# Layer 0's node stage of a four-layer graph network: rows normalized in x's order, and turned in four sets of 64 columns

## What is computed

```
h = jnp.maximum(_layernorm(x, axis=-1), 0.0)
s, v = h[:, :64], h[:, 64:].reshape(N, 64, 3)
f0, m0 = s @ W_li0, s @ W_lm0                         # scaled by node_vec1 / 8
f1 = einsum('num,uk->nkm', v, W_li1)                  # the same matrix for each of the 3 components m
m1 = einsum('num,uk->nkm', v, W_lm1)
f0, f1 = f0 / sqrt(deg), f1 / sqrt(deg)
```

## Time and profile before

| | us |
|---|---|
| median of 3 runs | 5679.57 |
| the profiled execution | 5676.4 |
| its span (first to last instruction) | 5674.6 |
| PE busy in the span | 4132.8 (73%) |
| DVE busy | 3918.7 (69%) |
| ACT busy | 2419.7 (43%) |
| POOL busy | 3698.6 (65%) |

### The profile page before, as it was taken

One profiled execution on the slowest core, in us unless ns is written; L12 is line 12 of the kernel. 1 busy time (PEld: TensorE's weight loads), 2 busy tenths in 40 slices (PEclk: granted clock), 3 DMA queues, 4 the chain that ended last, 5 costly groups with the idle time before them and its releaser, 6 DMA issues. The chain is left out here.

```text
span 5674.6 us, 77383 instructions
## 1 busy us (share of the span) xinstructions
PE 4132.8 (73%) x16540; PEld 2547.2 (45%) x16540; DVE 3918.7 (69%) x9333; ACT 2419.7 (43%) x6729; POOL 3698.6 (65%) x4307
## 2 busy tenths in 40 slices
PE   2699999999994565656567777777756666666688
PEld 2555555555573443434344444444434444444344
DVE  6699999999974555555545665565657676776653
ACT  3699999999952333333350000000113333333322
POOL 4477777777726777777737777777337777777300
PEclk8899999999997777777787887877887777778799
DMA  4643333333334555555533333333435555555331
GB/s 173 209 140 105 104 104 105 104 105 104 103 121 142 140 145 143 142 143 142 140 104 106 105 106 106 105 105 106 130 105 149 142 149 142 149 144 148 102 107 46
DMA packets 473229, 704.52 MB, mean 124 GB/s; under 512 B 203979, under 2 KB 313913, under 8 KB 472624
## 3 DMA queue, kind: packets, MB, share of 16 engines
q0 software_dynamic: 168848, 468.38, 29.6%
q1 hardware_dynamic: 297530, 224.65, 13.2%
q10 hardware_dynamic: 6416, 6.55, 0.3%
HBM read 619.63 MB, written 75.81 MB: 123 GB/s over the span
## 5 line engine op out<-in xcount | busy, mean ns | idle before, releaser
L273 POOL DMA_INDIRECT G<-table,srcI x1760 | 1674.6, 951 | 585.1 <-issue 500.9
L542 PE MATMUL pS<-G,one 128*128 128x260 f32 (+1 forms) x3520 | 1205.6, 481 | 192.6 <-issue 96.5
L1434 POOL DMA_INDIRECT G<-table,srcI x880 | 837.2, 951 | 332.3 <-ACT zt L1460 190.0
L475 ACT ACTIVATE acc<-pS x1760 | 691.2, 393 | 781.7 <-PE pS L542 532.1
L1571 PE MATMUL pM<-zt,one 128*128 128x512 f32 x1760 | 915.4, 601 | 75.5 <-DVE zt L1517 75.1
L626 POOL DMA_INDIRECT G<-table,srcT x831 | 787.3, 947 | 270.2 <-issue 129.5
L680 PE MATMUL pM<-G,one 128*128 x1760 | 657.0, 501 | 274.3 <-SPq L657 248.0
L1460 ACT ACTIVATE zt<-G,a4S 128x128 f32<-128x128 f32 x2640 | 856.3, 389 | 0.0
L542 PEld LDWEIGHTS pS<-G,one 128*128 128x128 f32 x3520 | 593.7, 212 | 264.6 <-issue 211.1
L1532 DVE TENSOR_TENSOR acc<-acc,pM 128x512 f32 x880 | 598.4, 680 | 51.1 <-PE pM L1571 51.0
L680 PEld LDWEIGHTS pM<-G,one 128*128 128x128 f32 x1760 | 374.0, 239 | 549.7 <-issue 504.5
(11 more groups left out here) (341 smaller groups left out, 5442.0 us busy)
## 6 DMA issues: line engine op xcount, KB each, us to landing
relT<-step_rel SPq DMA_DIRECT2D x220, 256.0 KB
G<-table,srcI POOLq DMA_INDIRECT x2640, 2.8
a10T<-step_a SPq DMA_DIRECT2D x660, 30.0 KB
far<-step_rec SPq DMA_DIRECT2D x224, 64.0 KB
G<-table,srcT POOLq DMA_INDIRECT x831, 2.8
table<-row SPq DMA_DIRECT2D x100, 128.0 KB, 1.7
acc<-zero SPq DMA_DIRECT2D x21, 512.0 KB, 5.1
step_a<-part SPq DMA_DIRECT2D x7, 960.0 KB, 3.9
```

The costliest lines, as they stand in the source:

```text
L273: pool.indirect_dma_start(G[:, par * C + j, 0:ROW], None, tab, bass.IndirectOffsetOnAxis(ap=srcI[:, k:k + 1], axis=0)).then_inc(s_g[par * ...
L475: nc.scalar.activation(tile(whole, to[j]), sum_of(of[j]), ACT.Copy).then_inc(s_out, 1)
L542: nc.tensor.matmul(sum_of(of[j]), one[:, par * C + j, :], G[:, par * C + j, :], start=False, stop=True, skip_group_check=True).then_inc(s_ ...
L1434: pool.indirect_dma_start(G[:, k % GS, :], None, table[0], bass.IndirectOffsetOnAxis(ap=srcI[:, k:k + 1], axis=0)).then_inc(s_g[k % GS], 16)
```

## The change

It touches layer 0 alone. ScalarE normalizes a tile's 256 columns in one operation, in x's order, as the other layers do. TensorE turns four sets of 64 columns (s; then each component, whose columns are 3 elements apart) to 64 lanes; pT and yT are 64 lanes by 512 columns, node n of set q at column 128 q + n. VectorE copies all 512 columns of the 64 lanes. TensorE multiplies each set by li and by lm, eight products over 64 rows with 64 moving columns. The results lie in pO as before, so the ends are as they were. w0 is 64 lanes with four matrices of 64 x 64, loaded by four DMAs.

```diff
-                yT = [st.sb(f"yT{j}", [P, D]) for j in range(NY)]
+                lanes_of, across = (P, D) if blocks is None else (MUL, 4 * P)
+                yT = [st.sb(f"yT{j}", [lanes_of, across]) for j in range(NY)]
...
-                pT = [st.ps(f"pT{j}", [P, D]) for j in range(2)]
+                pT = [st.ps(f"pT{j}", [lanes_of, across]) for j in range(2)]
...
-                            if blocks is not None:
-                                ins = blocks.norm(y[j], tile(x_sb, n), n)
-                            else:
-                                ins = nc.scalar.activation(y[j][:, :], tile(x_sb, n), ACT.Relu, bias=shift[:, ds(n, 1)], scale=rstd[:, ds(n, 1)])
-                            ins.then_inc(s_y, 1)
+                            nc.scalar.activation(y[j][:, :], tile(x_sb, n), ACT.Relu, bias=shift[:, ds(n, 1)],
+                                                 scale=rstd[:, ds(n, 1)]).then_inc(s_y, 1)
...
-                            for c in range(2):
+                            if blocks is not None:
+                                ins = blocks.turn(pT[j], y[j])
+                            for c in range(2 if blocks is None else 0):
                                 ins = nc.tensor.transpose(pT[j][:, c * P:(c + 1) * P], y[j][:, c * P:(c + 1) * P], ident[:, :])
...
-                w0 = st.sb("w0", [P, 2, 2, P])
+                w0 = st.sb("w0", [MUL, 2, 2, MUL])
...
-                            for f, (first_of, other) in enumerate((("L0_gnn_W_li0", "L0_gnn_W_li1"), ("L0_gnn_W_lm0", "L0_gnn_W_lm1"))):
-                                for c, half, name in ((0, 0, first_of), (0, 1, other), (1, 0, other), (1, 1, other)):
-                                    at = slice(half * MUL, half * MUL + MUL)
-                                    sp.dma_start(w0[at, c, f, at], a[name]).then_inc(s_w1, 16)
+                            for f, names in enumerate((("L0_gnn_W_li0", "L0_gnn_W_li1"), ("L0_gnn_W_lm0", "L0_gnn_W_lm1"))):
+                                for i, name in enumerate(names):
+                                    sp.dma_start(w0[:, f, i, :], a[name]).then_inc(s_w1, 16)
...
-                            sp.wait_ge(s_w1, 128)
+                            sp.wait_ge(s_w1, 64)
...
-                    def norm(self, y, xt, n):
-                        scaled = dict(bias=shift[:, ds(n, 1)], scale=rstd[:, ds(n, 1)])
-                        nc.scalar.activation(y[:, 0:MUL], xt[:, 0:MUL], ACT.Relu, **scaled)
-                        return nc.scalar.activation(y[:, MUL:D].rearrange("p (m k) -> p k m", m=3),
-                                                    xt[:, MUL:D].rearrange("p (k m) -> p k m", m=3), ACT.Relu, **scaled)
+                    def turn(self, pT, y):
+                        for q in range(4):
+                            part = y[:, 0:MUL] if q == 0 else y[:, MUL + q - 1:D:3]
+                            ins = nc.tensor.transpose(pT[:, q * P:(q + 1) * P], part, ident[:, :])
+                        return ins
 
                     def multiply(self, pO, yT):
-                        for c in range(2):
+                        for q in range(4):
                             for f in range(2):
-                                ins = nc.tensor.matmul(pO[f][:, c * P:(c + 1) * P], yT[:, c * P:(c + 1) * P], w0[:, c, f, :], start=True, stop=True)
+                                ins = nc.tensor.matmul(pO[f][:, q * MUL:(q + 1) * MUL], yT[:, q * P:(q + 1) * P], w0[:, f, min(q, 1), :],
+                                                       start=True, stop=True)
```

## The result

The changed kernel takes 5799.7 us (median of 4 runs, 5796.8 to 5803.4) against 5678.2 before: ratio 1.0212, 95% interval 1.0199 to 1.0225, **slower by 121 us**. The forecast was +29, and the range ended at 5730. The profiled execution's span is 5800.7 us.

A forecast was written before the change was run, and what follows sets the result against it. With no engine full before, TensorE was to become the bound at 2.25 us a tile: 112.5 + 5.5 start + 17 lowest parts + 5 clock = 140 us against 111.4, +29, so 5708 us; range 5690 to 5730.

The forecast's parts named there:

- the fourth line of the sum, the clock: Node stage: after gaps, three stretches of 3.3 us at half clock, 5 us (none: 0; all seven: 12).
- the rival named for it: Node stage: every gap costs 6.6 us at clock 0.50, 23 us instead of 5, giving 5726 us; chance 0.15.
- a sign that the prediction is wrong: Node stage: the granted clock being well under the 0.85 of today would refute the prediction.
- Products: TensorE, node stage: 16 pairs instead of 8 at 0.111 us each, +0.89 us a tile at full clock.
- The 50-column row of the preparation: Edge count in the preparation: 16 pairs, 50 moving columns, 0.111 us each; taken as the price of a smaller pair.
- Rows don't count: TensorE's weight loads: one row took 319 ns against up to 338 for 128 rows at half clock.
- Turns: TensorE: four transposes of 64 columns instead of two of 128, +0.22 to 0.27 us a tile, twice that at half clock.
- VectorE's copy: Copy of the turned rows: 512 elements a lane instead of 256, 0.66 us instead of 0.42, +0.24 us.
- Normalization: ScalarE: one operation over 256 columns, a form taking 587 ns, replaces two; -0.52 us a tile.
- Each lowest part, 17 us together: VectorE's lowest parts of blocks: TensorE stalls 2.35 us five times, 1.2 + 1.45 for the last two.
- The rival by moving columns: TensorE's products: a 64-column pair costs 0.056 us, so products stay at 0.89 us a tile; +5, 5685 us; chance 0.11.
- faster: Node stage: ScalarE's lateness is the path, additions are hidden, 28 waits each 0.52 us shorter; -14, 5665 us; chance 0.03.

The follow-up runs named there:

- e1: Kernel before, each of layer 0's four products issued twice (16 load-and-product pairs a tile, 128 rows by 128 columns): 5685.1 us, ratio 1.0016.
- e2: Kernel before, each product of 128 moving columns split into two of 64 over all 128 rows (16 pairs a tile): 5754.4 us, ratio 1.0133.
- e3: Kernel before, each product issued twice over the first 64 rows only, 128 moving columns (16 pairs a tile): 5783.5 us, ratio 1.0185.
- e6: Kernel before with the change's product shape alone, eight products of 64 rows by 64 columns; turns, copy, normalizations as before: 5779.1 us, ratio 1.0187.
- e9: Changed kernel with four more unused full-size products (8 pairs, 128 rows by 128 columns) in each tile: 5753.1 us, ratio 1.0137.
- e5: Changed kernel with 24 unused full-size products (48 pairs) on TensorE at the start of the node stage, a warm start: 5788.3 us, ratio 1.0203.
- e7: Kernel before with the change's single normalization over 256 columns alone; turns and products as before: 5655.4 us, ratio 0.9968.
- e8: Change's normalization and turns, but the kernel before's products; turned sets packed onto 128 lanes by VectorE and ScalarE copies: 5673.1 us, ratio 1.0001 against before.

## Why the prediction was wrong

The step that failed is the fourth line of the sum, the clock: 5 us, with an end of 12, and 23 in the rival named for it. All three price the clock by gaps. The argument against more was that TensorE would be busier than before, and that in the last tiles, busy all the time, its clock was 1.00. Those tiles' products are of 128 rows and 128 columns. The changed kernel is busy for 112.6 of 113.6 us at 0.50, which was named as a sign that the prediction is wrong; e1 is busy for 85.5 of 96.0 us at 1.00. So busy time did not hold the clock up. With pairs of 128 rows and 128 columns it was up (e1), with fewer rows or columns, turns and normalization as before, it was down (e2, e3, e6), and in e9, with pairs of the first kind added, it came up after six tiles and stayed. At the higher clock a tile of the change takes 2.56 us (e9), so the clock's part is 50 x (4.59 - 2.56) = 102 of the 119 us. The Trainium skill, page "TensorE: Matmul & The Clock Gate", section "Part 1: The HAM clock gate (the "warmup" mystery)", says that the default is the lower clock and that activity releases it; read as the profile's busy time, these runs contradict it. What the chip counts as activity stays open.

The other steps, by the order of the sum:

- *Products.* Right. The first 16 loads in e5 are (1.86 - 0.188) / 15 = 0.111 us apart over 64 rows, with 0.188 as the length of one load at the higher clock (the median in e9), and at the lower clock (3.49 - 0.330) / 15 = 0.211. The 50-column row of the preparation was the right one to price by. "Rows don't count" holds for a load's length (330 against 333 ns).
- *What was priced at nothing.* A change of the number of rows between turns and products holds up the next load: 0.49 us a tile at the lower clock (e6 against e2). At the higher an estimate is 2.56 - 2.25 = 0.31, what e9 measured less the forecast's sum. The rows of before could not show it; there all of the stage is 128 rows.
- *Turns.* Right: four at (1.06 - 0.42) / 3 = 0.21 us at the lower clock, strided loads of 177 ns under them.
- *VectorE's copy.* 0.66 forecast, 0.68 measured. *Normalization.* 587 forecast, 588 measured, and off the path of the changed kernel.
- *Each lowest part, 17 us together.* Wrong, with the other sign: TensorE never waited for one. They took 1.47 us instead of 3.3, as GpSimd's subtraction, whose start depends on VectorE's bn_stats, no longer ran beside them, and at 4.59 us a tile there was time for them anyway. No run shows what they would cost the change at the higher clock. The duration of a row was taken over to a kernel in which its neighbour has moved.
- *The rival by moving columns* (5685) and *faster* (5665) are excluded by the loads' spacing. But where nothing is added, -0.52 us a tile on ScalarE went with 17 us (e7), not the 5 to 8 that the sum's way of counting gave; how much of it is the shorter lowest parts' is not separated.

With 2.56 us a tile, 4 us of slow start and no gap, the change would have cost an estimated 50 x 2.56 + 4 - 111.4 = 21 us at the higher clock. That is near the forecast 29 by luck: the sum has 17 us of gaps too much and 15 us of row changes too little. The direction was right by its mechanism, TensorE as the bound through twice the loads; the size was the clock's.

## What to carry to other kernels

When a matmul is cut into smaller ones, price the number of weight loads, and look for a row of the trace where pieces of that shape ran for a while, and at what clock: here half the rows or half the columns kept a whole stage at half speed. Price the stretch at both clock levels, and give the lower one a chance of its own even if the engine will be busy without a gap. Before a duration is taken from a trace, look at which other engine was working at that time: here an operation on VectorE that met GpSimd's took up to 2.6 times its own length.

## What was not expected of the hardware

- 128 rows with 64 columns, 64 rows with 128, and 64 with 64, each 16 pairs a tile, ran at the lower clock for the whole stage (0.50 for 64 with 64; loads of 333 and 330 ns for the other two); 128 with 128 ran at 1.00. Small pairs didn't hold the clock that large ones had brought up (e5: 1.00 until 138.9 us, with the first product over 64 rows at 135.6).
- Adding 8 large pairs to each tile made the stage faster by 39 us and the kernel by 47 (e9).
- A load with another number of rows than the work before it starts late: 0.49 us at the lower clock for both directions together (e6 against e2).
- VectorE's subtraction of 1280 f32 into bf16 took 1.47 us alone and up to 3.88 beside GpSimd's subtraction. It can go the other way too: where VectorE got ahead, GpSimd's operation was the longer one (e7: 1.60 instead of 0.20; e8: 4.15 instead of 2.62).
